# Four graph layers on one core: layer 3's chain of small steps, and where the self loop is added

## What is computed

```python
# layer 2
adj_hat = adj + eye
out = relu(d[:, None] * adj_hat * d[None, :] @ (h @ W) + b)      # d = rowsum(adj_hat) ** -0.5
# layer 3
norm(v) = max(sqrt(sum(v * v)), EPS)
log0(y) = arctanh(clip(norm(y), 0, MAX_TANH)) * y / norm(y)
exp0(v) = tanh(norm(v)) * v / norm(v)
h_add(x, y) = ((1 + 2xy + y2) * x + (1 - x2) * y) / max(1 + 2xy + x2 * y2, EPS)   # xy, x2, y2: row dots
h2    = h_add(exp0(log0(h) @ embed), embed_bias)
neigh = exp0(adj @ log0(h2))
out   = h_add(exp0(log0(concat(h, neigh)) @ layer), layer_bias)
```

## Time and profile before

| | us |
|---|---|
| median of three runs | 900.39 |
| the profiled execution, its own time | 900.15 |
| its span, first to last instruction | 898.4 |
| TensorE busy | 844.8 |
| VectorE busy | 644.3 |
| ScalarE busy | 473.4 |
| GpSimd busy | 290.0 |

### The profile page before, as it was taken

The page is one execution under the profiler, slowest core; times in us unless marked ns, Lnnn a source line. Parts: engine busy times, 40 slices in busy tenths (PEclk is TensorE's granted clock), DMA queues, the critical chain, the costliest instruction groups (busy, mean ns, idle before and its releaser), DMA issues.

```text
span 898.4 us, 18058 instructions
## 1 busy us (share of the span) xinstructions
PE 844.8 (94%) x6368; PEld 505.3 (56%) x6368; DVE 644.3 (72%) x1784; ACT 473.4 (53%) x987; POOL 290.0 (32%) x381
## 2 busy tenths in 40 slices
PE   0699999999999999999999999999999999999992
PEld 0366777777777777654444445554555555555441
DVE  6989999999999999962545434433147666637876
ACT  5878888887888887741111101101055665434543
POOL 6844444444554465531212100000022131213221
PEclk9899999999999999999999999999999999999997
DMA  8999999999999996000011100000000000000000
GB/s 264 225 220 265 240 267 234 291 227 246 266 268 258 238 255 119 2 1 7 18 24 23 24 1 1 1 1 1 0 1 1 1 1 1 1 1 24 24 24 24
DMA packets 104783, 91.87 MB, mean 102 GB/s; under 512 B 83072, under 2 KB 88320, under 8 KB 104704
## 3 DMA queue, kind: packets, MB, share of 16 engines
q1 hardware_dynamic: 101056, 90.20, 42.9%
q10 hardware_dynamic: 3648, 0.61, 0.4%
HBM read 69.81 MB, written 2.10 MB: 80 GB/s over the span
## 4 chain that ended last, share of the span: by engine, by line
PE 70%; DVE 16%; issue 6%; ACT 3%; DVEq 2%; POOL 2%; DMA 1%; ACTq 0%; SPq 0%; POOLq 0%
PE ps_acc L1374 28%; PE ps_acc L1293 16%; PE ps_s L1276 10%; PE ps_t L1374 6%; PE ps_t L1276 5%; DVE e_parts L806 3%; DVE ps_s L799 2%; POOL att_sb L398 1%; ACT e_parts L615 1%; DVE adj_t L738 1%; PE ps_s L1404 1%; PE ps_s L1436 1%; DMA x<-in_x 1%; DVE adj_t L755 1%; ACT ez L584 1%
## 5 line engine op out<-in xcount | busy, mean ns | idle before, releaser
L347 POOL CAST e_parts<-ez 128x512 f16<-128x512 f32 x256 | 158.8, 648 | 177.0 <-ACT ez L496 115.7
L1293 PEld LDWEIGHTS ps_acc<-h_a,e_parts 128*128 128x128 f16 x3072 | 185.9, 97 | 34.0 <-DVE e_parts L806 4.0
L1293 PE MATMUL ps_acc<-h_a,e_parts 128*128 128x129 f16 x3072 | 197.4, 219 | 2.3 <-DVE e_parts L806 2.1
L1374 PE MATMUL ps_acc<-adj_t,stage 128*128 128x512 fp8e4 x896 | 198.6, 379 | 0.0
L806 DVE TENSOR_TENSOR e_parts<-ez,e_parts 128x512 f16<-128x512 f32 x256 | 179.4, 740 | 1.0 <-POOL e_parts L347 1.0
L1374 PE MATMUL ps_acc<-adj_t,h_a 128*128 128x512 fp8e4 x768 | 169.0, 379 | 0.0
L584 ACT ACTIVATE ez<-x,small 128x128 f32 (+1 forms) x96 | 39.5, 482 | 202.8 <-DVE small L985 202.8
L1374 PEld LDWEIGHTS ps_acc<-adj_t,stage 128*128 128x128 f16 x896 | 87.1, 98 | 99.1
L1276 PE MATMUL ps_s<-u_t 128*128 128x512 f16 x534 | 132.9, 386 | 8.9 <-ACT ez L496 7.2
L471 ACT ACTIVATE bytes<-stage 128x1024 uint8<-128x1024 f32 x128 | 133.8, 1045 | 0.9 <-DVE x L767 0.6
L496 ACT ACTIVATE ez<-ps_s,scal 128x1024 f32<-128x1024 f32 x89 | 107.2, 1204 | 44.8 <-DVE ps_s L799 43.6
(11 more groups left out here) (161 smaller groups left out, 795.7 us busy)
## 6 DMA issues: line engine op xcount, KB each, us to landing
stage<-in_adj SPq DMA_DIRECT2D x128, 512.0 KB, 5.0
x<-in_x SPq DMA_DIRECT2D x4, 512.0 KB, 8.2
adj_t<-bytes SPq DMA_TRANSPOSE x128, 5.3
out<-x SPq DMA_DIRECT2D x8, 256.0 KB, 2.2
u_t<-e_parts SPq DMA_TRANSPOSE x16, 2.4
kernel_sb<-in_L_gnn_kernel ACTq DMA_DIRECT2D x1, 64.0 KB, 7.0
w_sb<-in_L_gnn_W ACTq DMA_DIRECT2D x1, 64.0 KB, 8.2
embed_top<-in_L_gnn_embed ACTq DMA_DIRECT2D x1, 64.0 KB, 8.3
```

Source lines behind the costliest of these rows:

```text
L347: g.tensor_copy(e_parts[:, HI, at, :], ez[:, at, :]).then_inc(ehi_done, 1)
L1293: last = t.matmul(att_acc[:, b, 0:D + 1], e_parts[:, re, g_s % RING, P * b:P * (b + 1)], h_a[:, s, rh, 0:D + 1], start=(s == 0 and n == 0 ...
L1374: last = t.matmul(acc, h[:, k, r, :], adj_f8[:, k // 2, CW * c:CW * (c + 1), k % 2], start=(k == 0 and r == LO), stop=(k == NB - 1 and r = ...
```

## The change

Four edits.

1. The self loop of layer 2: the eight matmuls per chunk go. Instead GpSimd adds `ident16x2` into the four diagonal blocks of chunk m's adjacency, after layer 1's aggregation of that chunk and behind its `rstd`, and takes it out again after layer 2's aggregation, in `roots_of_pair` between the roots of v and of h2. TensorE waits for it at the quarter that reads those blocks. GpSimd's loop over pairs is written out.
2. ScalarE runs a logarithm of a constant behind tanh of n_a in each part of layer 3.
3. `atanh_begin` takes a function called after four of its steps; layer 3 gives it the dot products, and their order and output buffer change.
4. `exp_map_add` multiplies tanh into one factor first and uses that twice (also in layer 2's loop); the same is done with cat_sq in layer 3.

```diff
+            def self_loops(m, op, done):
+                for b in range(BC):
+                    k = BC * m + b
+                    own = adj_f8[:, k // 2, P * k:P * (k + 1), k % 2]
+                    last = g.tensor_tensor(own, own, ident16x2[:, :], op, saturate=False)
+                last.then_inc(done, 1)
             with pool.Fori(0, NCH) as m:
                 rstd(NCH + m)
+                pool.wait_ge(agg_done, NCH + m + 1)
+                self_loops(m, ALU.add, loop_in)
 ...
                 for par in (0, 1):
                     root_v(2 * i + par, par)
                 for par in (0, 1):
+                    pool.wait_ge(agg_done, 2 * NCH + 2 * i + par + 1)
+                    self_loops(2 * i + par, ALU.subtract, loop_out)
+                for par in (0, 1):
                     root(of_chunk(h2_sq, par), of_chunk(n_h2, par), h2_sq_in, n_h2_ok,
 ...
-            with pool.Fori(0, NCH // 2 - 1) as i:
+            for i in range(NCH // 2 - 1):
                 roots_of_pair(i)
 ...
                 tanh_step(NCH // 2 + 2 * k + 1, n_a[:, cut], cut)
+                a.activation(ln_first, half, ACT.Ln)
 ...
-            def atanh_begin(n, factor, cut=PAIR):
+            def atanh_begin(n, factor, cut=PAIR, between=lambda step: None):
 ...
                 v.tensor_scalar(at_u[:, cut], at_t[:, cut], 1.0, None, ALU.add).then_inc(ln_in, 1)
+                between(0)
                 dve.drain()
                 v.scalar_tensor_tensor(at_w[:, cut], at_u[:, cut], -1.0, n[:, cut], ALU.add,
                                        ALU.mult)
+                between(1)
                 dve.drain()
                 v.reciprocal(at_w[:, cut], at_w[:, cut])
+                between(2)
                 dve.drain()
                 v.scalar_tensor_tensor(at_w[:, cut], at_t[:, cut], 0.5 * factor, at_w[:, cut],
                                        ALU.mult, ALU.mult)
+                between(3)
                 dve.drain()
 ...
+                dve.wait_ge(tanh_out, k_tanh)
+                v.tensor_tensor(th_q[:, cut], th_q[:, cut], th[:, cut], ALU.mult)
+                dve.drain()
                 v.scalar_tensor_tensor(th_a[:, cut], v_y[:, cut], 2.0, th_q[:, cut], ALU.mult,
                                        ALU.mult)
                 v.tensor_tensor(th_x[:, cut], v_sq[:, cut], th_q[:, cut], ALU.mult)
                 dve.drain()
-                v.tensor_tensor(th_x[:, cut], th_x[:, cut], th_q[:, cut], ALU.mult)
-                dve.drain()
-                dve.wait_ge(tanh_out, k_tanh)
-
-                v.tensor_tensor(th_q[:, cut], th_q[:, cut], th[:, cut], ALU.mult)
-                v.tensor_tensor(th_a[:, cut], th_a[:, cut], th[:, cut], ALU.mult)
-                v.tensor_tensor(th_x[:, cut], th_x[:, cut], th[:, cut], ALU.mult)
-                dve.drain()
-                v.tensor_tensor(x2[:, cut], th_x[:, cut], th[:, cut], ALU.mult)
                 v.tensor_scalar(a_c[:, cut], th_a[:, cut], 1.0, None, ALU.add)
+                v.tensor_tensor(x2[:, cut], th_x[:, cut], th_q[:, cut], ALU.mult)
                 dve.drain()
 ...
-                v.tensor_tensor(cat_sq[:, cut], r_a[:, cut], r_a[:, cut], ALU.mult)
-                dve.drain()
-                v.tensor_tensor(cat_sq[:, cut], cat_sq[:, cut], a_sq[:, cut], ALU.mult)
-                dve.drain()
                 dve.wait_ge(tanh_out, NCH // 2 + 2 * k + 1)
                 v.tensor_tensor(tq[:, cut], th[:, cut], r_a[:, cut], ALU.mult)
-                v.tensor_tensor(cat_sq[:, cut], cat_sq[:, cut], th[:, cut], ALU.mult)
-                dve.drain()
-
-                v.tensor_tensor(cat_sq[:, cut], cat_sq[:, cut], th[:, cut], ALU.mult)
-                dve.drain()
+                dve.drain()
+                v.tensor_tensor(cat_sq[:, cut], tq[:, cut], a_sq[:, cut], ALU.mult)
+                dve.drain()
+                v.tensor_tensor(cat_sq[:, cut], cat_sq[:, cut], tq[:, cut], ALU.mult)
+                dve.drain()
 ...
-                atanh_begin(n_cat, 1.0, cut)
-                dot_with(lb_bc, v_ok, 2 * i, pars)
+                dve.wait_ge(v_ok, 2 * i + pars[-1] + 1)
+                def dots(step):
+                    for par in pars:
+                        dot(lb_bc, BC * par + step, g_f[:, BC * par + step, :])
+                atanh_begin(n_cat, 1.0, cut, dots)
 ...
-                if L == 2 and q == NB // BC - 1:
-
-                    for b in range(BC):
-                        for r in (LO, HI):
-                            t.matmul(acc[:, P * b:P * (b + 1)], h[:, BC * c + b, r, :],
-                                     ident16x2[:, :], start=False, stop=False,
-                                     skip_group_check=True)
+                if L >= 2 and q == c:
+                    pe.wait_ge((loop_in, loop_out)[L - 2], c + 1)
```

More of the change, by code:

```diff
@@ L147, in program @@
         l1_bias_bc, l2_b_bc, eb_bc, lb_bc = (bias_bc[:, n, :] for n in range(4))
-        scal = sb("scal", [P, 12])
+        scal = sb("scal", [P, 13])
         (alpha_c, beta_c, e_alpha, sig_c, sig_h, x_coef, beta_s, shift_c, y2_embed, y2_layer,
-         neg_half, half) = (scal[:, n:n + 1] for n in range(12))
+         neg_half, half, ln_first) = (scal[:, n:n + 1] for n in range(13))
         deg_parts = sb("deg_parts", [P, NB, 4])
@@ L209, in program @@
                  "h_sq_in n_h_ok v_sq_in n_v_ok h2_sq_in n_h2_ok a_sq_in n_a_ok cat_sq_in "
-                 "n_cat_ok tanh_in tanh_out ln_in ln_out h2_ok v_ok v_out split_g beta_split beta_in "
+                 "n_cat_ok tanh_in tanh_out ln_in ln_out h2_ok v_ok v_out split_g loop_in loop_out beta_split beta_in "
                  "x_less x_att").split()
@@ L220, in program @@
          h_sq_in, n_h_ok, v_sq_in, n_v_ok, h2_sq_in, n_h2_ok, a_sq_in, n_a_ok, cat_sq_in,
-         n_cat_ok, tanh_in, tanh_out, ln_in, ln_out, h2_ok, v_ok, v_out, split_g, beta_split,
+         n_cat_ok, tanh_in, tanh_out, ln_in, ln_out, h2_ok, v_ok, v_out, split_g, loop_in, loop_out,
+         beta_split,
          beta_in, x_less, x_att) = (
@@ L409, in _ @@
                                 ).then_inc(bias_in, 1)
-            with pool.Fori(0, NCH) as m:
+            def self_loops(m, op, done):
[4 more added lines that the diff above has]
+                last.then_inc(done, 1)
+            for m in range(NCH):
                 rstd(NCH + m)
+                pool.wait_ge(agg_done, NCH + m + 1)
+                self_loops(m, ALU.add, loop_in)
             def root_h(m, par):
@@ L1077, in atanh_end, with dot, dot_with @@
                 dve.drain()
-            def dot_with(y, ready, count, pars=(0, 1)):
-                for par in pars:
+            def dot(y, b, spare):
+                v.scalar_tensor_tensor(spare, v0[:, b, :], 1.0, y, ALU.mult, ALU.mult,
+                                       accum_out=v_y[:, b:b + 1])
+            def dot_with(y, ready, count):
+                for par in (0, 1):
                     dve.wait_ge(ready, count + par + 1)
                     for b in range(BC * par, BC * (par + 1)):
-                        v.scalar_tensor_tensor(tmp[:, b % BC, :], v0[:, b, :], 1.0, y,
-                                               ALU.mult, ALU.mult, accum_out=v_y[:, b:b + 1])
+                        dot(y, b, tmp[:, b % BC, :])
                     dve.drain()
```

## The result

| | before | after |
|---|---|---|
| median of the runs on one chip, us | 900.59 (900.18 to 901.58, 12 runs) | 899.0 (898.12 to 900.33, 12 runs) |
| ratio after / before, 95% interval | | 0.9981 [0.9973, 0.9988] |
| profiled execution: time, span, us | 900.15, 898.4 | 899.43, 897.5 |

Predicted were 898.1 us and a range of 895.6 to 902.0. The change saves 1.6 us, 0.19%, just short of the 0.2% that the prediction took as the limit of what can be told from no change. (The diff shown above has layer 1's loop over `rstd` on GpSimd as unchanged context; the change writes that loop out too.)

A forecast was written before the change was run, and what follows sets the result against it. Layer 2 was taken as paced by a closed chain across engines, not TensorE's queue. Layer 2 -0.43, layer 3's middle -0.97 and tail -0.86 gave -2.3: 897.9 profiled, 898.1 us as median, range 895.6 to 902.0.

The forecast's parts named there:

- The closed chain: Layer 2: a loop of ScalarE, VectorE, GpSimd and `prepare`, without an aggregation, sets the period of 35.16 us per pair.
- P: Layer 2: start-to-start time of one 128x128 self-loop operation on GpSimd, taken as 0.31 us, between 0.25 and 0.6.
- C: Layer 2: loss per pair when GpSimd's eight subtractions hold up VectorE's chain, about 8P - 1.5, so 1.0 us.
- rival B: Layer 2: somewhat slower GpSimd, P 0.36 to 0.42, C 1.4 to 1.8; about 899.7 us; chance 0.17.
- Rival A: Layer 2: GpSimd and VectorE don't hinder each other, C = 0; sum -4.6, 895.8 us; chance 0.18.
- G: Layer 2: gain per call from the shorter `exp_map_add` on VectorE, 0.48 us.
- Chunk 3 and chunk 5: Layer 2: shifts of these chunks' `prepare` steps against the kernel before, -0.82 and -0.30 us, decided by the chain.
- Chunk 7: Layer 2: shift of the last odd chunk's `prepare`, -0.43 us from the chain, against -0.75 for TensorE alone.
- Layer 3's middle: Chunk 5: TensorE's wait of 0.97 us for ScalarE goes entirely, through the early logarithm and VectorE's shorter way.
- Tail: Last chunk of layer 3, set by VectorE: factor -0.30, logarithm -0.18, `exp_map_add` -0.38, together -0.86 us.
- D: Layer 3: squares bring another table in after the early logarithm, so the load stays; 898.6 us; chance 0.05.
- C, the other sign: Layer 2: byte operands at stride two make GpSimd slow, P = 0.5; sum +2.4, 902.8 us; chance 0.15.

The follow-up runs named there:

- no_loop: Kernel before without its 64 self-loop matmuls on TensorE and nothing in their place; ratio 0.9980.
- loops_only: Kernel before with only the self loops moved from TensorE to GpSimd, VectorE and ScalarE as before; ratio 1.0024.
- moved: Kernel after with each pair's eight GpSimd subtractions behind the first root of v instead of the second; 895.43 us, ratio 0.9944.
- old_exp_map: Kernel after with `exp_map_add` as it was before; 900.85 us, ratio 1.0004.
- evac_first: Kernel after with ScalarE's evacuation of the odd chunk's aggregation ahead of the pair's second logarithm in layer 2; 898.14 us, ratio 0.9974.
- unrolled_only: Kernel before with ScalarE's loop over the pairs of layer 2 written out, nothing else; ratio 0.9987.
- chain_only: Kernel before with everything of the change except the self loops, which stay on TensorE; ratio 0.9953.

## Where the prediction was right and where it was not

The time came out 0.9 us above the forecast, with its sign and inside its range; the gain of 0.19% is at the edge of what it called no change. Of the 0.9 us, 0.2 are the sum's (2.08 aligned for 2.26). Another 0.2 are the kernel before, 900.59 in twelve runs against 900.39 in three. The remaining 0.5 lie in the two groups of runs: six of the twelve runs after are in the later one, four of the twelve before. That the sum itself came so close is luck in good part, as its steps show:

**The closed chain: right, and the number rests on it.** no_loop shows it by itself. The start value of -1.34 was met by no_loop (-1.32) and, with C, by loops_only (-1.34 + 1.24 = -0.10; -0.12 measured).

**P was mis-sized, C less so.** P was taken as 0.31 and is 0.39 (an eighth of the 3.12), close to the 0.40 at which the sum was said to turn to zero. By the prediction's own formula, 8P - 1.5, that would have made C 1.6 and the time rival B's, 899.7. C came out at 1.24 to 1.25. The picture behind the formula was right: L1133 starts at 714.62, just behind GpSimd's end at 711.32 + 3.12 = 714.44. Its small terms were not. Hand-overs and last step were put at 0.45 and are 0.18; GpSimd starts 0.06 us ahead of VectorE, which the formula left out; the free chain was put at 1.92 and is 1.99 (moved). So C = 3.12 - 0.06 + 0.18 - 1.99 = 1.25, and a P too small by 0.08 (0.64 in eight) was more than half made good by terms too large by 0.40.

That the two engines exclude each other was read from the earlier trace rows, and the stretched chain fits it, but for the reciprocal. Rival A's case, C = 0, is nearly that of moved: 895.43 us, where A had said 895.8.

The Trainium skill's rule (page "SBUF — State Buffer", section "Who interferes with whom") agrees in kind: the two-input instructions and the TENSOR_SCALARs are stretched from 0.17 to 0.24 to 0.46, the reciprocal stays at 0.20 in both kernels. The Trainium skill's page "GPSIMD Engine Reference", section 3.1, had led to an estimate of 0.28 us for 128 elements. The rows say 0.38 start to start, and the measurement decides.

**G: the number right, by luck.** 0.48 predicted, 0.50 by the periods of old_exp_map and of moved against no_loop (35.16 - 34.65 = 0.51). But the prediction had all of it between L1098 and L1115, 1.61 to become 1.13. There it became 1.21 (moved, 710.30 to 711.51), a gain of 0.40; the other 0.1 is the pause ahead of L991, for which the sum had no term.

**Chunk 3 and chunk 5: the first right because two errors cancel.** -0.82 and -0.30 predicted, -0.81 and -0.08 measured. C was 0.25 larger and the function's own gain 0.08 smaller than taken; the pause ahead of L991 in the first pass gave 0.36 back: -1.34 - 0.40 - 0.36 + 1.25 = -0.85. From chunk 3 to 5 the sum -0.81 - 0.50 + 1.24 gives -0.07.

**The waits ahead of `prepare`: sum right, place wrong.** 1.9 and 1.7 were forecast, 1.00 and 0.99 measured. The rest, 0.62 each, stands ahead of the odd chunks' weights. I had asked what TensorE waits for next only at `prepare`, where it already waited, and not at the other steps that hang on ScalarE. evac_first puts the waits back together: 1.79 and 1.80.

**Chunk 7: the step that failed.** -0.43 predicted, +0.36 measured. With the measured terms the chain alone gives -0.08 - 0.50 + 1.24 - 0.65 = +0.01, and evac_first has +0.01 (to the hundredth by chance, as the scatter of 0.14 between like kernels shows). So of the error of 0.79, 0.44 is the mis-sized C - G (0.74 for 0.52, twice between chunks 3 and 7), and 0.35 is left for the wait of the weights, for which the sum had no term; evac_first against the kernels with that wait puts it at 0.3. The prediction took "TensorE alone" as its queue without waits of its own.

**Layer 3's middle: gain right, cause in part wrong.** The 0.97 went entirely: from `prepare` of chunk 7 to the transposes the time fell by 1.13, and by 1.19 to the product behind them (853.21 against 852.86), which now starts 0.44 us after them instead of 0.50. The prediction gave this to the early logarithm and VectorE's shorter way together; without the early logarithm it goes too. It stays in no_loop, loops_only and unrolled_only (0.96 to 0.99), which have VectorE's old layer 3. It is gone in every kernel with the shorter factor, also where one of early logarithm, dots between the steps and new `exp_map_add` is undone. So no single one of these three is needed. Which of them would suffice alone, or the factor alone, was not tried.

**Tail.** Row by row, kernel after:

```profile
883.67 0.18 DVE L1218 RECIPROCAL att_sb<-att_sb 128x4 f32<-128x4 f32 x1
...
884.64 0.17 DVE L1227 TENSOR_TENSOR att_sb<-att_sb,cols 128x4 f32<-128x4 f32 x1
...
887.06 0.17 DVE L1077 TENSOR_SCALAR att_sb<-att_sb 128x4 f32<-128x4 f32 x1
...
888.85 0.16 DVE L1095 TENSOR_TENSOR att_sb<-att_sb 128x4 f32<-128x4 f32 x1
...
889.84 0.16 DVE L1120 TENSOR_TENSOR att_sb<-att_sb 128x4 f32<-128x4 f32 x1
...
890.95 0.22 DVE L1133 SCALAR_TENSOR_TENSOR att_sb<-att_sb,scal 128x4 f32<-128x4 f32 x1
...
892.26 1.14 DVE L1254 SCALAR_TENSOR_TENSOR x<-bias_bc,att_sb,x 128x128 f32<-128x128 f32 x4
```

Against the earlier trace rows: the factor 0.97 for 1.27, -0.30 as predicted; logarithm and dots 1.79 for 2.02, -0.23 (predicted -0.18); `exp_map_add` 1.11 for 1.49, -0.38 as predicted. Between them 0.07 is lost. And 0.35 was in no term: the kernel before stood idle ahead of its last additions, with no other engine as the cause. The kernel after has such a pause too, but ahead of an earlier chunk's additions (before, then after):

```profile
893.17 1.14 DVE L1235 SCALAR_TENSOR_TENSOR x<-bias_bc,att_sb,x 128x128 f32<-128x128 f32 x4 [0.43 <-issue]
```

```profile
879.72 0.16 DVE L1142 TENSOR_TENSOR att_sb<-att_sb 128x4 f32<-128x4 f32 x1 [0.45 <-issue]
```

There it costs nothing, since VectorE afterwards waits 1.02 us for GpSimd (883.41). So this third of the tail's gain is no work saved; a pause fell elsewhere, which nothing in the prediction could tell.

**The sum.** Predicted -0.43 - 0.97 - 0.86 = -2.3; measured +0.36 - 1.13 - 1.19 = -1.96. To -2.08 there are 0.12 more: 0.06 between the transposes at chunk 5 and the product behind them, and 0.06 between the last transposes and the tail's first step (880.45 to 883.41, before 880.10 to 883.12). An error of 0.8 in layer 2 was nearly made good by 0.6 elsewhere, and more than half of that 0.6 is the pause of the tail.

**The rivals.** A fell with the chain of 3.24 us, C with P below 0.40. B had its P (0.39) but not its C. D fell too: by line, the 13 table loads at L635 became seven at L649, all in layer 2, and six at L707, and the rows of chunk 4 above show L649 without a load. C, the other sign, did not come, but its mechanism is what made loops_only slower.

## What to carry to other kernels

Before work is moved off the busiest engine, look at the period of its waits: if two of them are exactly as far apart as a chain on the other engines, the freed time comes back as waiting, and only what shortens that chain counts. Before work is given to an idle GpSimd, ask what VectorE does in the same microseconds; the same eight operations cost 1.25 us per pair behind one root and next to nothing behind the other. And when a chain becomes longer, go through everything that is queued behind its waits on each in-order engine, here an evacuation behind a logarithm.

## What the runs showed of the hardware that I had not expected

- TensorE gives back more than its bracket shows when a wait vanishes: 0.67 for 0.49 and 0.51 for 0.25 (chunks 3 and 5, chain_only), 1.13 for 0.97 (chunk 5 of layer 3). The group behind a wait is listed with 1.99 us instead of 1.89.
- VectorE has idle times of 0.43 to 0.46 us named "issue", with no engine as the cause. In layer 3's second half two of them stand at 856.05 and 893.17 in the kernel before and at 859.46 and 879.72 in the kernel after: they move when the code changes, and whether they cost anything depends on where they fall. The one of 0.44 at 692.01 has no counterpart in the kernel after. What they are was not tried.
- With a hardware loop on ScalarE each pass begins with a table load of 1.28 us, and the logarithm behind it needs another from the second pass on; the written-out loop has neither (28 loads become 23 over the kernel).
- GpSimd adds a 128x128 fp8 block with a stride of two bytes to a 128x128 identity in 0.43 us, and the next one starts after 0.38.
